# Scatter of attention's rows into expert slots: indirect DMAs that write, or that add to zeros

## What is computed

```python
# attention (per head, in order of time t):
#   S_t = S_{t-1} + k_t (beta_t * (v_t - k_t^T S_{t-1}))^T ;  o_t = q_t^T S_t
x = _layernorm(x + attention(x))
# experts
expert_weights = jax.nn.softmax(x @ gate_w.T, axis=1)
_, selected_experts = jax.lax.top_k(expert_weights, 2)
# count: running number of choices of each expert; kept where count <= capacity
dispatch = jnp.einsum('bsm,bsec->ebcm', hidden_states, dispatch_mask)
expert_out = w2(silu(dispatch @ w1) * (dispatch @ w3))
final = jnp.einsum('ebcm,bsec->bsm', expert_out, combine_mask)
x = _layernorm(x + final)
```

## Time and profile before

| | |
|---|---|
| median of 3 runs | 681.89 us (678.12 to 695.77) |
| the profiled execution | 689.21 us, span 687.0 us |
| busy in the span | PE 555.2 us (81%), DVE 348.5 (51%), ACT 324.1 (47%), POOL 361.1 (53%) |
| the chain that ended last | PE 52%, POOL 13%, DMA 8%, "issue" 8%, "another core or an unknown queue" 7%, DVE 6% |
| attention part | up to about 450 us of the span |

### The profile page before, as it was taken

How to read it: one execution, slowest core, us unless ns; L and a number is a source line. 1 busy time by engine, 2 the same in 40 slices (tenths; PEclk the granted TensorE clock), 3 DMA queues, 4 the chain that set the end, 5 groups by cost and what they waited for, 6 DMA issues and landing times.

```text
span 687.0 us, 18848 instructions
## 1 busy us (share of the span) xinstructions
PE 555.2 (81%) x6852; PEld 423.5 (62%) x6852; DVE 348.5 (51%) x1337; ACT 324.1 (47%) x893; POOL 361.1 (53%) x697
## 2 busy tenths in 40 slices
PE   6538999889889889889888877359999997898920
PEld 4315666456556556556555655259999987898820
DVE  4014456554556555555555756435555635665613
ACT  2215664454454455455455444334645553454514
POOL 2056575556465455557447542304676764766770
PEclk9858998897797897889789887569999998999975
DMA  8913221230230230230231120323656545756534
GB/s 228 380 22 38 28 37 29 45 53 10 44 54 10 45 53 11 44 53 20 36 53 23 33 48 17 97 96 76 147 90 131 103 63 131 160 101 107 83 38 133
DMA packets 134861, 50.96 MB, mean 74 GB/s; under 512 B 89984, under 2 KB 127360, under 8 KB 134784
## 3 DMA queue, kind: packets, MB, share of 16 engines
q1 hardware_dynamic: 119776, 35.10, 23.3%
q0 software_dynamic: 13568, 9.51, 10.2%
q10 hardware_dynamic: 1440, 5.33, 1.9%
HBM read 26.63 MB, written 23.28 MB: 73 GB/s over the span
## 4 chain that ended last, share of the span: by engine, by line
PE 52%; POOL 13%; DMA 8%; issue 8%; another core or an unknown queue 7%; DVE 6%; ACT 3%; ACTq 1%; SPq 1%; POOLq 0%; DVEq 0%
POOL x_store L1569 11%; PE ps L635 5%; PE ps L650 5%; PE ps L643 4%; PE ps L888 4%; DMA x_store<-xk,row 4%; PE ps L902 3%; PE ps L621 3%; PE ps L707 2%; PE ps L809 2%; PE ps L628 2%; PE ps L719 2%; PE ps L675 2%; PE ps L629 2%
## 5 line engine op out<-in xcount | busy, mean ns | idle before, releaser
L1569 POOL DMA_INDIRECT x_store<-xk,row x80 | 127.0, 1587 | 88.4 <-issue 35.8
L1525 POOL TENSOR_TENSOR prod<-a,xs 64x15 f32<-64x15 f32 (+7 forms) x240 | 63.4, 264 | 140.6 <-DVE xs L1268 123.1
L1539 POOL DMA_INDIRECT slots_in<-x,slot x64 | 63.5, 992 | 53.0 <-DVE x L1350 36.7
L888 PE MATMUL ps<-xeTh,w13h 128*128 128x320 f32 x224 | 74.6, 333 | 15.8 <-DVE hb L1394 13.3
L1394 DVE TENSOR_TENSOR hb<-ps,hs 128x320 f32<-128x320 f32 (+1 forms) x128 | 61.5, 490 | 30.7 <-ACT hs L1089 25.7
L1526 POOL TENSOR_TENSOR xs<-xs,prod 64x15 f32<-64x15 f32 (+7 forms) x240 | 65.6, 273 | 18.8
L902 PE MATMUL ps<-w2s,hb 128*128 128x128 f32 x640 | 74.1, 275 | 0.0
L902 PEld LDWEIGHTS ps<-w2s,hb 128*128 128x128 f32 x640 | 72.8, 192 | 0.0
L888 PE MATMUL ps<-xeTh,w13l 128*128 128x320 f32 x224 | 71.5, 319 | 0.0
L888 PE MATMUL ps<-xeTl,w13h 128*128 128x320 f32 x224 | 71.3, 318 | 0.0
L1089 ACT ACTIVATE hs<-ps 128x320 f32<-128x320 f32 (+1 forms) x128 | 54.2, 435 | 34.8 <-PE ps L888 27.0
(11 more groups left out here) (194 smaller groups left out, 1100.3 us busy)
## 6 DMA issues: line engine op xcount, KB each, us to landing
w<-w_in SPq DMA_DIRECT2D x16, 448.0 KB
slots_in<-zeros ACTq DMA_DIRECT2D x10, 520.0 KB, 7.0
xe<-slots_in SPq DMA_DIRECT2D x16, 325.0 KB
w2s<-w SPq DMA_DIRECT2D x16, 192.0 KB
xTs<-xT SPq DMA_DIRECT2D x4, 512.0 KB, 6.1
xk<-x SPq DMA_DIRECT2D x4, 512.0 KB, 10.9
a_diag<-A SPq DMA_DIRECT2D x64, 32.0 KB
inv<-xs SPq DMA_DIRECT2D x16, 128.0 KB
```

What stands on the lines that cost most here:

```text
L888: last = mm(ps[:, HB[fill % 5], 0:HALF], w_[:, P * c:P * c + P], x_[:, par, cols], start=(t == 0), stop=(t == 2))
L1525: link(g.tensor_tensor(pr_, bc(a16[:, j + 1:, j], 2, j + 1), bc(xs[:, 0, j, 0:j + 1], 1, m), ALU.mult))
L1539: g.indirect_dma_start(out=xs_d[:, :], out_offset=bass.IndirectOffsetOnAxis(ap=to, axis=0), in_=x1[:, p % 2, j, k, :], in_offset=None).the ...
L1569: g.indirect_dma_start(out=x1_d[:, :], in_=ye[:, par, i, :], in_offset=None, out_offset=bass.IndirectOffsetOnAxis(ap=row[:, par, i:i + 1], ...
```

## The change

The four indirect DMAs of `scatter` get `compute_op=ALU.add`: they read the row in HBM, add to it and write it back, where they wrote it before. The slots hold zeros, so the values are the same. The spare rows, which got no zeros before, now get them too, by one more DMA from ACT behind the pass p = 4, and the first scatter waits for 11 of these DMAs where it waited for 10.

```diff
+                if p == 4:
+                    act.dma_start(xs_d[ROWS:ROWS + SPARE, :].rearrange("(p r) d -> p (r d)", p=P),
+                                  zeros[:, 0:SPARE // P * W]).then_inc(xs_zero, 16)
...
                 if p == 0:
-                    pool.wait_ge(xs_zero, 16 * XS_ZEROS)
+                    pool.wait_ge(xs_zero, 16 * (XS_ZEROS + 1))
...
                         g.indirect_dma_start(out=xs_d[:, :], out_offset=bass.IndirectOffsetOnAxis(ap=to, axis=0),
-                                             in_=x1[:, p % 2, j, k, :], in_offset=None).then_inc(scat[p % 2], 16)
+                                             in_=x1[:, p % 2, j, k, :], in_offset=None, compute_op=ALU.add
+                                             ).then_inc(scat[p % 2], 16)
```

## The result

The changed kernel took **627.4 us** (median of four runs, 620.19 to 630.30) beside 682.0 us for the kernel before (four runs, 678.12 to 695.77): a ratio of 0.9146, with a 95% interval of 0.9085 to 0.9207. Some executions fall into a slower state, and since medians take in all runs and ratios leave those out, a ratio isn't quite the quotient of the two medians. The kernel is 8.5% faster where 5% slower was forecast. The rival "no hold with adds" had forecast 629 us. Its profiled execution took 630.3 us, with a span of 628.1 against 687.0.

What follows compares the result with a forecast made beforehand. It took the hold of PE's small-tile results during POOL's scatters as what matters. Growing holds 33.6, end of attention 2.8 and zeroing 0.7 summed to 37.1 us: 719 us on the median of 681.9, range 680 to 742.

Steps and rivals of the forecast that it cites:

- no hold with adds: Rival: only plain writes hold PE back, so all 14 holds go, 57.2 us; 629 us on the median, chance 0.18.
- The hold: In attention steps, PE's small-tile results reach their readers late while POOL issues scatters; claimed on the path in nearly every step.
- Its price, 57.2 us: DVE's unnamed waits in attention: 12 for 50.4 us ahead of L1221, 2 for 6.8 us ahead of L1230.
- If its end moves with POOL's DMAs, each hold grows by 2.4 us: 14 x 2.4 = 33.6 us.: Likeliest case, chance 0.62: four longer adds per attention step lengthen each of 14 holds, 33.6 us in all.
- The far end: Rival: holds follow the adds' landing, growing 3.3 us each (46.2), and the clock falls further (24); 755 us, chance 0.03.
- POOL's idle 7.26 us covers the adds: Ahead of the next solve, POOL's idle time was to absorb the 2.4 us that four adds lengthen each step.
- The end of attention: The last scatter, on the path: three longer DMAs add 1.8 us and the later landing 1.0, together 2.8 us.
- The eleventh zeroing: ACT's extra DMA: its 1.2 us of issue hidden, its data costing 0.7 us, with 0 and 1.9 as ends.
- The rival built on it: Rival: the hold keeps its length, so only 3.5 us remain; 685 us on the median, chance 0.17.

Runs made afterwards that it cites:

- the hand-over kernel: Separate program, no layer: PE and DVE pass a small result every 0.65 us while POOL issues DMAs; four plain writes first delayed them 2.2 us in sum.
- the spaced writes: The kernel before with a waited copy of 64 x 256 elements on POOL behind each of the four plain writes: 617.8 us, ratio 0.906; 613.2 us in a later set.

## Why the prediction was wrong

**The hold as the bound: right.** The prediction found it from the unnamed waits, put 57.2 us on it, and kept it apart from whole-array matmuls; the hand-over kernel bears that out where they run alone. Behind small pieces they are held too: head_sums (L794) is a whole-array matmul, and ACT read it 4.3 us late. Beside 64 x 64 pieces the hand-over kernel showed no delay, but the changed kernel shows 0.6 us at L707, and plain writes with unwaited copies left ACT waiting up to 2.5 us there. That the hold isn't there on every occasion could not be seen from one trace.

**Its price, 57.2 us: too low.** Between sets with and without the hold the same kernel differs by 86 us. In the step of the earlier trace rows PE was idle for only 25.36 - 22.47 = 2.9 of the 6.5 us by which it is longer; the other 3.6 are longer busy time at the lower clock and added work, not the 1.7 that the prediction left for them. (From the matmul's end to DVE's copy it is 4.86 us; 4.75 is DVE's idle time.)

**"If its end moves with POOL's DMAs, each hold grows by 2.4 us: 14 x 2.4 = 33.6 us." This step failed.** It took the hold for one thing that lasts from PE's matmul to a microsecond behind the fourth DMA. It behaves like a row of short ones that run together when the starts are 1.28 to 1.36 us apart (682.0 and 684.8 us), only in some steps at 1.54 (623.5 us), and at 1.88 leave 0.6 to 1.2 us. The same 0.6 us per DMA that seemed to make it longer opened gaps between them. That each short one belongs to one DMA is read from the hand-over kernel's sections with copies; what makes it isn't shown. The term was -69.6 us between first and last scatter, not +33.6. The argument "its end has a steady place behind POOL's last DMA" came from four writes at a single distance, 1.3 us, and holds for those; a trace that has only one distance can't tell a length from an interval. The 0.62 on that case was too much for an operation that no row showed beside a small-tile matmul. The far end's 3.3 us is a wrong sum besides: a hold that follows the landing would grow by 1.8 + 1.0 = 2.8 us, as the prediction itself has it for the end of attention.

**The rival at 629: right in its number, only half right in its reason.** It supposed that plain writes alone hold PE back; the spaced writes refute that. Its bound was well worked out: POOL's 20.5 us a step was measured at 19.9 in the mean, and its upper end of 68 us for the steps was 69.6 between first and last scatter. That 629 came so close is luck in part: it took 57.2 us for the steps, and left out most of the 7.9 us lost ahead of the first scatter.

**POOL's idle 7.26 us covers the adds: right only beside the hold.** With the hold gone, that idle time is gone too: PE's own step is 18.24 us (L635 starts at 118.66, 136.89 and 155.13 in the chain of the kernel before without the hold). The first twelve steps took 219.7 us there and 240.0 in the changed kernel without the hold, 1.7 us more each, 20.4 in all, of the 32.4 us between the two spans (593.5 and 625.9). The prediction called POOL no bound and priced the adds on its queue at nothing. That cover was the stall itself.

**The end of attention, +2.8 us: right.** The last group takes 5.65 us from its first start to its last, where it took 4.15, and the last add lands 3.35 us behind its start where the write took 2.27: 1.5 + 1.1 = 2.6 us. The 2.8 us measured above from the last scatter's start to the end are not the same thing; 1.7 of them lie behind the landing and aren't explained. Block 14's group was not out of the way, though: POOL went from it to the last one with 1.43 us between.

**The eleventh zeroing, +0.7 (up to 1.9): a little low.** 2.5 us in the set that measured it. The first scatter started 7.9 us later in the changed kernel (7.1 in the sets without the hold), at a clock of 0.83 from 60 to 100 us where the kernel before had 0.96 (1.00 without the hold). Other kernels with the same zeroing started between 96.2 and 100.1 us, at 0.93 to 1.00, so that isn't the zeroing alone; what lowers the clock there wasn't tested.

**The Trainium skill's rule.** "SBUF — State Buffer", section "Who interferes with whom", says that DMA never contends with a compute engine and that PE and ACT never wait on anyone. It says so of the ports to SBUF, and no run here shows that the hold has to do with those. The sets without the hold agree with it: ACT read 0.05 us behind PE with three writes around it. Taken for results in general, as the prediction took it, it doesn't hold in the others: ACT waited 4.48 us. The rival built on it, 685 us, fell.

## What to carry over

Where a wait has no releaser in the profile, find out how it depends on the distance of the things beside it before pricing a change in their length: four DMAs 1.3 us apart held for 3 to 5 us in nearly every step, four 1.54 us apart in a few. Work of the same queue that has to be done anyway, put between small indirect DMAs (0.4 us each sufficed here), won in the sets with the hold and cost nothing in the others, and kept the plain write's price of 0.97 us instead of the add's 1.57. Slack on an engine beside a stall is not slack: work out the step's length without the stall (18.24 us here) before calling an engine's added work free.

## What was not expected of the hardware

- Results of PE's small-tile matmuls, and of a whole-array one right behind them, reached DVE and ACT up to 5.0 us late while POOL issued four indirect DMAs 1.27 to 1.36 us apart, in four sets of seven; in the others, the same program showed none of it and took 596 us instead of 682 to 687. No row names a cause.
- The add needs 1.57 us of POOL instead of 0.97, and what POOL starts behind it is slow too: silu of 128 x 256 elements took 1.30 us behind an add and 0.73 behind a write, and the first `prod` behind that 0.80 instead of 0.21.
- A single indirect DMA of either kind, and a single plain one with one or three copies behind it (not waited for), delayed none of the hand-overs, which came every 0.65 us.
